# A vision-transformer layer on one core: the class product of the class query's weighted sum moved behind the four token products

## The chip, the cores and the metric

One core of a Trainium2 chip runs the whole program. The metric is the device time of one execution in microseconds; the median of several executions is compared.

## The reference

Sixteen images of 512 tokens with 256 features pass through one layer. The changed lines belong to the attention, whose core is, cut to what matters:

```python
h = concatenate([broadcast(cls_tok), tok(x)], axis=1)      # 513 rows an image
...
q, k, v = bitlinear(x, w_q), bitlinear(x, w_k), bitlinear(x, w_v)   # 16 heads of 16
scores = einsum('bhqd,bhkd->bhqk', q, k) * SCALE
attn = softmax(scores, axis=-1)
out = einsum('bhqk,bhkd->bhqd', attn, v)
...
h = h + bitlinear(out, w_o)
h = h + moe_top2(layernorm(h))                              # 8 experts
```

The class token is row 0 of each image. As a query it attends to the 512 tokens and to itself. Its output is a sum over 512 token keys and one class key, weighted by exponentials of the scores, divided by the sum of the weights.

## The kernel before

The program has two large parts. The first, which the change touches, takes the images through a software pipeline: gate and up projections, attention, router. The second goes over the experts' token lists and follows behind a barrier.

In the first part five images are in flight. One turn of the pipeline has 64 steps (four groups of four heads, 16 units each; `at` counts the steps, `u` the units of a group). In a turn the functions `body` of the engines hand over `T, P, C, W, X`: image T is in the token projections, P in the attention's projections, C in the score maxima, W at the end of its attention, X in the output projection and the router. The order of the work on each engine is written out by hand by these step numbers; the engines wait for each other through semaphores alone. Turns 3 to 12 are a hardware loop with two turns in its body, the others are straight code.

Each step of `tensor_program` begins with a score product of 512 keys (`score_unit`, line 493), whose row maximum VectorE takes (`head_max`, line 1147) into `mxs`, and a transposed score product (`scoret_unit`, line 502), whose exponential ScalarE takes into `pt` (line 823). The score products alternate between two PSUM banks, so TensorE can be one or two units ahead of VectorE. The attention's products `pv` (line 511) come every fourth step: four heads, each with 32 output columns, write the four strips of 32 partitions of one bank.

At step 35 the class query's weighted sum of image W stands (lines 737 to 743). `pc` holds the exponentials: 32 columns (16 heads and padding) for each of four tiles of 128 tokens, and in place `TB` one row for the class key. `v_sb` holds the values of a tile, 16 heads by 32 columns, `vcls` those of the class token. The product of token tile t goes into partitions 32t to 32t + 31 of PSUM bank `d2`; the class key's product, of one row, is added into the strip of tile 0. All are float32, and each is executed in two passes (two records in the trace). The last of the five raises `pe_pvc`.

```python
for t in range(TB):
    last = mm(d2[VW * t:VW * (t + 1), :], pc[:, W.par, t, :], ...)
    if t == 0:
        mm(d2[0:VW, :], pc[0:1, W.par, TB, :], vcls[0:1, W.par, :, :]...)
last.then_inc(s("pe_pvc"), 1)
```

At step 36 VectorE, behind its row maximum, waits for `pe_pvc` and multiplies the whole bank by the mask `diagonal` into `pvd` (line 1436). TensorE's transposes of the attention's output into the same bank, `d2`, wait for that at step 38 (line 635). At step 44 line 750 sums the four strips. On VectorE step 35 also has a piece of the router of image X (lines 1241 to 1243, on masks `rtmp` and `oh`), at step 41 another (lines 1241 to 1246) and at step 42 the router's weights (lines 1255 to 1257). GpSimd runs the low parts of the queries and keys of image P by step numbers of its own: line 1021 and line 1025 at step 35, line 1029 at step 42, each some 2 us.

Of the kernel before, what the change touches and what calls it, by code (L numbers as in the profile page):

```python
# [19 lines left out]
TB = S // 128  # L20
# [6 lines left out]
VW = 32  # L27
# [70 lines left out]
def fresh(eng, at, *batches):  # L98

    if batches[0].n is None or isinstance(batches[0].n, int):  # L100
        return batches
    n = batches[0].n
    copy = eng.alloc_register(f"lap_{batches[0].k}_{at}")
    eng.reg_mov(copy, n)
    n = eng.snap(copy, min_val=n.min_val, max_val=n.max_val)
    return [At(b.k, n, b.ok) for b in batches]


def wait(eng, sem, per, b, n):

    value = b.v * per + n
    if not isinstance(value, int) or value > 0:
        eng.wait_ge(sem, value)
# [31 lines left out]
def token_phase(nc, outer, images, x_t, cls, w0_t, w1_t, wo_t, attn_w_t, gate_w, consts, out,  # L145
# [12 lines left out]
    def s(name):  # L158

        if name not in sems:  # L160
            sems[name] = nc.alloc_semaphore(f"{name}_{stage}")
        return sems[name]
# [101 lines left out]
    vcls = sb("vcls", [128, 2, NH, VW])  # L264
# [4 lines left out]
    pc = sb("pc", [128, 2, TB + 1, VW])  # L269
# [51 lines left out]
    d0, d1, d2 = banks[5:8]  # L321
# [143 lines left out]
    def tensor_program(pe, stage):  # L465
        mm, tr = nc.tensor.matmul, nc.tensor.transpose
        if stage == SETUP:
# [8 lines left out]
            for c in range(DC):  # L476
                last = mm(d1[:, 4 + c:5 + c], cls_norm[:, blk(c)], ones[0:1, 0:1], start=True, stop=True)
# [37 lines left out]
        def body(T, P, C, W, X):  # L515
            for g in range(NG):
                for u in range(UNITS):
                    if u % 4 == 0:
                        T, P, C, W, X = fresh(pe, UNITS * g + u, T, P, C, W, X)
# [10 lines left out]
                    if T.ok and at in GATE_AT:  # L530
# [10 lines left out]
                        for c in range(DC):  # L541
                            last = mm(d0[:, :], w0[:, c, blk(e)], xt[:, T.par, c, :], start=(c == 0), stop=(c == DC - 1))  # L542
                        last.then_inc(s("pe_gate"), 1)
                    if T.ok and at in UP_AT:
# [7 lines left out]
                        for c in range(DC):  # L552
                            last = mm(d1[:, :], w1[:, c, blk(e)], xt[:, T.par, c, :], start=(c == 0), stop=(c == DC - 1))
                        last.then_inc(s("pe_up"), 1)
                    if T.ok and at in OUT_AT:
                        t = OUT_AT.index(at)
# [4 lines left out]
                        for e in range(EC):  # L561
                            last = mm((d0, d1)[t // 2][:, D * (t % 2):D * (t % 2 + 1)], hid[:, e, blk(t)], wo[:, e, :],
                                      start=(e == 0), stop=(e == EC - 1))
                        if t % 2:
                            last.then_inc(s("pe_h"), 1)
                    if C.ok and at == 0:
# [4 lines left out]
                        for c in range(DC):  # L571
                            mm(d2[:, 0:D], xq[:, c, S:SEQ].broadcast_to([128, 128]), wq_int[:, 2, c, :],
                               start=(c == 0), stop=(c == DC - 1))
                        for w in range(2):
                            for f in range(DC):
                                for c in range(DC):
                                    last = mm(d2[:, D + 2 * w + f:D + 2 * w + f + 1], wq_int[:, w, c, blk(f)],
                                              xq[:, c, S:SEQ], start=(c == 0), stop=(c == DC - 1))
                        last.then_inc(s("pe_cols"), 1)
                    if X.ok and at == 1:  # L580
# [5 lines left out]
                        for c in range(DC):  # L586
                            for t in range(TB):
                                last = tr(b16(d0)[:, c * S + t * 128:c * S + (t + 1) * 128], qi2[:, t, blk(c)], id_bf[:, :])
                        last.then_inc(s("pe_xq2"), 1)
                        tr(b16(d1)[0:64, 0:NG], qic[:, :], id_bf[0:NG, 0:NG]).then_inc(s("pe_xqc"), 1)  # L590
                    if C.ok and at == 3:
# [3 lines left out]
                        for k, (a, o) in enumerate(((fq, kbd), (fk, qbd))):  # L595
                            for half in range(2):
                                for c in range(DC):
                                    last = mm(d2[VW * (2 * k + half):VW * (2 * k + half + 1), 0:S // 2], o[:, c, :],
                                              a[:, c, half * S // 2:(half + 1) * S // 2], start=(c == 0), stop=(c == DC - 1))
                        last.then_inc(s("pe_ct"), 1)  # L600
                    if X.ok and at in (4, 5):
# [5 lines left out]
                        for t in (2 * k, 2 * k + 1):  # L607
                            for c in range(DC):
                                last = mm((d0, d1)[k][:, D * (t % 2):D * (t % 2 + 1)], xq2[:, c, blk(t)],
                                          wq_int[:, 3, c, :], start=(c == 0), stop=(c == DC - 1))  # L610
                            last.then_inc(s("pe_y"), 1)
                    if u == 6 and tg[0].ok:
# [21 lines left out]
                        for t in range(TB):  # L634
                            last = tr(d2[:, blk(t)], pvs[:, blk(t)], identf)
                        last.then_inc(s("pe_tg"), 1)
                    if u == 9 and mt[0].ok:
# [8 lines left out]
                        for t in range(TB):  # L646
                            last = tr(b16(d2)[0:MROWS * GH, blk(t)], nmp[:, t, :], id_bf[:, :])
                        last.then_inc(s("pe_mt"), 1)
                    if P.ok and at == 10:
                        wait(pe, s("act_xh"), TB, P, TB)  # L650
                        wait(pe, s("dve_sst"), 1, P, 1)
                        if X.ok:
                            wait(pe, s("dve_h2"), TB, X, TB)
                        mm(d1[:, 0:2 * TB], ones[:, :], sums1[:, :, :].rearrange("p a t -> p (a t)"),
                           start=True, stop=True).then_inc(s("pe_st1"), 1)
                    if C.ok and at == 12:
# [6 lines left out]
                        for c in range(DC):  # L663
                            last = mm(d2[:, S // 2:S // 2 + NH], fq[:, c, S:SEQ].broadcast_to([128, 128]),
                                      kbd[:, c, 0:NH], start=(c == 0), stop=(c == DC - 1))
                        wait(pe, s("dve_cm"), 1, C, 1)
                        mm(d2[:, CM_AT:CM_AT + 2 * VW], cm[:, 0:1].broadcast_to([128, 128]), cst[:, C_ID + 2 * VW:C_ID + 4 * VW],
                           start=True, stop=True).then_inc(s("pe_t7"), 1)
                    if X.ok and at == 9:
                        hold(pe, s("dve_h2"), TB, X, 2)  # L670
                        for k in range(NG):
                            last = mm(d0[0:1, 0:D], xqc[:, k:k + 1], wo_cls[:, k, :], start=(k == 0), stop=(k == NG - 1))
                        last.then_inc(s("pe_yc"), 1)
                    if P.ok and at == 24:
# [5 lines left out]
                        for t in range(TB):  # L680
                            last = mm(d1[:, blk(t)], aq1[:, t:t + 1].broadcast_to([128, 128]), identf, start=True, stop=True)
                        last.then_inc(s("pe_aqb"), 1)
                    if P.ok and at == 23:
# [5 lines left out]
                        for c in range(DC):  # L689
                            for t in range(TB):  # L690
                                last = tr(b16(d0)[:, c * S + t * 128:c * S + (t + 1) * 128], qi[:, t, blk(c)], id_bf[:, :])
# [8 lines left out]
                    if X.ok and at in (28, 30):  # L700
# [9 lines left out]
                        for t in range(TB):  # L710
                            last = tr(d2[:, blk(t)], x2[:, t, blk(c)], identf)
# [3 lines left out]
                    if P.ok and at in (41, 42):  # L715
# [7 lines left out]
                        for t in (2 * k, 2 * k + 1):  # L723
                            for c in range(DC):
                                last = mm((d0, d1)[k][:, D * (t % 2):D * (t % 2 + 1)], xq[:, c, blk(t)],
                                          wq_int[:, 2, c, :], start=(c == 0), stop=(c == DC - 1))
# [3 lines left out]
                    if W.ok and at == 35:  # L730

                        wait(pe, s("act_pc"), 1, W, 1)
                        if X.ok:
                            wait(pe, s("dve_lg"), 1, X, 1)
                        else:
                            wait(pe, s("act_mt"), NG, C, 1)
                        for t in range(TB):
                            last = mm(d2[VW * t:VW * (t + 1), :], pc[:, W.par, t, :],
                                      v_sb[:, W.par, t, :, :].rearrange("p h w -> p (h w)"), start=True, stop=(t > 0))
                            if t == 0:  # L740
                                mm(d2[0:VW, :], pc[0:1, W.par, TB, :], vcls[0:1, W.par, :, :].rearrange("p h w -> p (h w)"),
                                   start=False, stop=True)
                        last.then_inc(s("pe_pvc"), 1)
                    if W.ok and at == 44:

# [3 lines left out]
                        for k in range(NG):  # L749
                            last = mm(d2[0:NG, 0:GH * VW], cst[:, C_SEL + k * NG:C_SEL + (k + 1) * NG],  # L750
                                      pvd[:, k * GH * VW:(k + 1) * GH * VW], start=(k == 0), stop=(k == NG - 1))
# [9 lines left out]
                    if W.ok and at == 56:  # L761
# [4 lines left out]
                           start=True, stop=True).then_inc(s("pe_amc"), 1)  # L766
# [31 lines left out]
        if stage == STEPS:  # L798
            steps(pe, body)
# [1058 lines left out]
```

## Time and profile before

| | |
|---|---|
| three runs | 2411.87, 2416.78, 2420.08 us (median 2416.78) |
| profiled execution | span 2410.7 us; no time of its own beside the span is listed |
| granted TensorE clock, mean | 0.955 |
| TensorE busy | 2081.0 us (86%) |
| VectorE busy | 1571.5 us (65%) |
| ScalarE busy | 1210.0 us (50%) |
| GpSimd busy | 911.2 us (38%) |

The span runs from the first to the last instruction of the program. Lines L1 to L1857 are the lines of the kernel. PE is TensorE, DVE VectorE, ACT ScalarE, POOL GpSimd. A timeline gives the start of an instruction, its duration, engine, line, operation, what it writes and reads, the shapes, and in brackets how long the engine sat idle ahead of it and what ended that. Instructions of one line in a row are merged (x2, x8). Matmuls overlap, so their cost is read from start to start. A granted clock of 1.00 is 2.4 GHz, 0.50 is 1.2 GHz.

### The profile page before, as it was taken

What the parts mean: (1) busy time and instruction counts of PE and PEld (TensorE: products, weight loads), DVE (VectorE), ACT (ScalarE), POOL (GpSimd) and SP (SyncE); (2) the same over time, 40 slices, a digit from 0 to 9 for tenths busy, and PEclk for the clock granted to TensorE, in tenths of its full rate; (3) what the DMA queues carried; (4) which work ended last, traced back from release to release, by engine and by line L of the source; (5) the groups of instructions that cost most, each with busy time, mean ns of one, the idle gap of its engine ahead of it and who ended that gap; (6) DMA issues with size and microseconds to landing.
All of it is one profiled execution on the core that took longest, in us unless ns stands there. A gap on an engine that the chain in (4) does not pass through costs nothing. (4 is left out here: it accounts for less than half of the span.)

```text
span 2410.7 us, 46759 instructions
## 1 busy us (share of the span) xinstructions
PE 2081.0 (86%) x11964; PEld 1058.4 (44%) x12049; DVE 1571.5 (65%) x4036; ACT 1210.0 (50%) x2360; POOL 911.2 (38%) x894
## 2 busy tenths in 40 slices
PE   4889999999898898998998988861099999999997
PEld 2433444444343444443444433321066666666665
DVE  3477888887887887887888898841633333333332
ACT  1256566566565565665656666640444444444443
POOL 2222242332423423333234244133245555555554
PEclk9899999999999999999999998985599999999999
DMA  2322332322222323223232232201523333333332
GB/s 99 83 74 53 86 87 69 93 71 81 85 71 68 87 69 88 77 70 87 69 78 82 65 85 74 64 27 45 191 45 57 53 56 54 53 56 52 55 54 37
DMA packets 181071, 171.97 MB, mean 71 GB/s; under 512 B 40002, under 2 KB 169620, under 8 KB 180884
## 3 DMA queue, kind: packets, MB, share of 16 engines
q1 hardware_dynamic: 150612, 134.94, 20.1%
q0 software_dynamic: 30272, 34.80, 9.1%
q8 instruction: 86, 1.41, 0.3%
q14 instruction: 101, 0.83, 0.2%
HBM read 100.82 MB, written 68.93 MB: 70 GB/s over the span
## 5 line engine op out<-in xcount | busy, mean ns | idle before, releaser
L1147 DVE TENSOR_REDUCE mxs<-bank 128x1 f32<-128x512 f32 x1024 | 697.1, 685 | 205.0 <-PE bank L493 186.5
L823 ACT ACTIVATE pt<-bank 128x512 f32<-128x512 f32 x1024 | 588.5, 593 | 388.8 <-PE bank L502 369.3
L493 PE MATMUL bank<-ks,qs 96*128 96x512 bf16 x1024 | 397.9, 390 | 84.1 <-DVE mxs L1147 53.3
L502 PE MATMUL bank<-qs,ks 99*128 99x512 bf16 x1024 | 393.4, 385 | 9.2 <-ACT pt L823 8.7
L1697 POOL DMA_INDIRECT out<-y_sb,ids x136 | 214.6, 1578 | 273.3 <-DMA out<-y_sb,ids 193.7
L511 PE MATMUL bank<-pt,v_sb 128*32 128x512 f32 x2048 | 278.0, 615 | 0.0
L493 PEld LDWEIGHTS bank<-ks,qs 96*128 96x128 bf16 x1024 | 103.1, 101 | 357.5 <-DVE mxs L1147 214.0
L1826 DVE TENSOR_TENSOR hl<-bank,hh 128x512 bf16<-128x512 f32 x136 | 94.1, 692 | 210.7 <-ACT hh L1796 210.7
L1822 DVE TENSOR_TENSOR hid_e<-bank,act_g 128x512 f32<-128x512 f32 x136 | 94.1, 692 | 210.5 <-PE bank L1743 209.0
L974 POOL DMA_INDIRECT list_dram<-pay,slot_i x130 | 138.3, 1064 | 240.9 <-DVE pay L1272 206.7
L1743 PE MATMUL bank<-gu_l,xh 128*128 x544 | 206.9, 380 | 22.9 <-issue 21.2
L1743 PE MATMUL bank<-gu_h,xl 128*128 x543 | 206.6, 380 | 0.0
L991 POOL TENSOR_TENSOR cadd<-vcls,pr 128x256 f32<-128x256 f32 x64 | 41.1, 642 | 400.3 <-DVE pr L1194 400.0
L1743 PE MATMUL bank<-gu_h,xh 128*128 x477 | 181.9, 381 | 2.0 <-issue 1.2
L1688 POOL DMA_INDIRECT xg<-x_dram,ids x136 | 135.8, 998 | 64.7 <-issue 36.9
L1728 PE MATMUL bank<-dn_h,hh 128*128 x544 | 148.4, 273 | 3.0 <-DVE hl L1826 1.6
L1728 PE MATMUL bank<-dn_h,hl 128*128 x544 | 148.3, 273 | 0.0
L1728 PE MATMUL bank<-dn_l,hh 128*128 x544 | 148.3, 273 | 0.0
L502 PEld LDWEIGHTS bank<-qs,ks 99*128 99x128 bf16 x1024 | 100.2, 98 | 98.8 <-issue 38.6
L1789 ACT ACTIVATE act_g<-bank 128x512 f32<-128x512 f32 x136 | 81.2, 597 | 122.8 <-PE bank L1743 121.9
L542 PE MATMUL bank<-xt,w 128*128 128x512 f32 x256 | 130.8, 635 | 7.7 <-DMA xt<-x_t 7.7
L1784 ACT ACTIVATE y_sb<-bank,ids 128x256 f32<-128x256 f32 x136 | 64.3, 473 | 141.5 <-PE bank L1728 121.7
(283 smaller groups left out, 3529.2 us busy)
## 6 DMA issues: line engine op xcount, KB each, us to landing
qs<-qk_dram SPq DMA_DIRECT2D x128, 128.0 KB, 2.6
ks<-qk_dram SPq DMA_DIRECT2D x64, 192.0 KB, 3.4
xt<-x_t SPq DMA_DIRECT2D x16, 512.0 KB, 4.2
h_dram<-h_sb SPq DMA_DIRECT2D x16, 512.0 KB
qs<-qk_dram SPq DMA_DIRECT2D x128, 64.0 KB, 2.2
ks<-qk_dram SPq DMA_DIRECT2D x64, 128.0 KB, 3.4
hw<-h_dram SPq DMA_DIRECT2D x16, 512.0 KB, 4.3
out<-hw SPq DMA_DIRECT2D x16, 512.0 KB, 2.9
```

Of the source, the lines that this page charges most:

```text
L493: mm(score[u % 2][:, :], qs[0:QK, h, blk(t)], ks[0:QK, h, :], start=True, stop=True) \
L502: mm(scoret[u % 2][:, :], ks[0:QK + MROWS, h, blk(t)], qs[0:QK + MROWS, h, :], start=True, stop=True).then_inc(s("pe_st"), 1)
L511: last = mm(pv_bank[VW * j:VW * (j + 1), :], v_sb[:, b.par, t, g * GH + j, :], pt[:, t % 2, j, :], start=(t == 0), stop=(t == TB - 1))
L542: last = mm(d0[:, :], w0[:, c, blk(e)], xt[:, T.par, c, :], start=(c == 0), stop=(c == DC - 1))
L823: f(pt[:, t % 2, j, :], scoret[u % 2][:, :], ACT.Exp).then_inc(s("act_exp"), 1)
L974: g_.indirect_dma_start(out=list_dram, out_offset=bass.IndirectOffsetOnAxis(ap=slot_i[0:np_, k, t:t + 1], axis=0), in_=pay[0:np_, k, t, :] ...
L1147: v.reduce_max(mxs[:, t, g * GH + j:g * GH + j + 1], score[u % 2][:, :], AX.X).then_inc(s("dve_mx"), 1)
L1688: nc.gpsimd.indirect_dma_start(out=xg[:, i.place(ROWS), :], out_offset=None, in_=x2_dram, in_offset=rows(i)) \
L1697: nc.gpsimd.indirect_dma_start(out=out, out_offset=rows(i), in_=y_sb[:, i.place(2), :], in_offset=None, bounds_check=tokens - 1, oob_is_er ...
L1728: last = mm(y_b[:, 0:D], a[:, i.place(2), c, :], w[:, bass.ds(e, 1), c, :], start=(n == 1), stop=(n == 3 * FC))
L1743: last = mm(bank[k][:, :], a[:, k, c, :], w[:, bass.ds(e, 1), c, lo:lo + F], start=(m == 1), stop=(m == 3 * DC))
L1822: v.tensor_tensor(hid[:, :], up_b[i.place(2)][:, :], act_g[:, :], ALU.mult).then_inc(dve_hid, 1)
```

## The change

The class key's product is issued after the four token products instead of after the first, and raises `pe_pvc` in place of the product of tile 3. Operands, shapes and the accumulation flags of each product stay.

```diff
                         for t in range(TB):
                             last = mm(d2[VW * t:VW * (t + 1), :], pc[:, W.par, t, :],
                                       v_sb[:, W.par, t, :, :].rearrange("p h w -> p (h w)"), start=True, stop=(t > 0))
-                            if t == 0:
-                                mm(d2[0:VW, :], pc[0:1, W.par, TB, :], vcls[0:1, W.par, :, :].rearrange("p h w -> p (h w)"),
-                                   start=False, stop=True)
+                        last = mm(d2[0:VW, :], pc[0:1, W.par, TB, :], vcls[0:1, W.par, :, :].rearrange("p h w -> p (h w)"),
+                                  start=False, stop=True)
                         last.then_inc(s("pe_pvc"), 1)
```

On TensorE, at steps 35 and 36 in the loop's body, before (L738 is the token products, L741 the class product, L104 and L113 are bookkeeping of the loop's registers):

```order
L511 MATMUL bank<-pt,v_sb 32x512 x4
L738 MATMUL bank<-v_sb,pc 32x512
L741 MATMUL bank<-vcls,pc 32x512
L738 MATMUL bank<-v_sb,pc 32x512 x3
L104 ISA
L493 MATMUL bank<-ks,qs 128x512
L113 REGISTER_ALU
L502 MATMUL bank<-qs,ks 128x512
```

and with the change (lines behind the edit have moved up by one, the class product is L740):

```order
L511 MATMUL bank<-pt,v_sb 32x512 x4
L738 MATMUL bank<-v_sb,pc 32x512 x4
L740 MATMUL bank<-vcls,pc 32x512
L104 ISA
L493 MATMUL bank<-ks,qs 128x512
L113 REGISTER_ALU
L502 MATMUL bank<-qs,ks 128x512
```

The four token products now stand together behind the four of the attention, and the class product stands between them and the score product of step 36.

On TensorE in the last image, where no score products are left, before (L780 is the router's logits, L635 the transposes that wait for `pvd`):

```order
L780 MATMUL bank<-gate_sb,x_t 128x8 x8
L511 MATMUL bank<-pt,v_sb 32x512 x4
L738 MATMUL bank<-v_sb,pc 32x512
L741 MATMUL bank<-vcls,pc 32x512
L738 MATMUL bank<-v_sb,pc 32x512 x3
L635 MATMUL bank<-cst,pvs 128x128 x4
```

and with the change:

```order
L779 MATMUL bank<-gate_sb,x_t 128x8 x8
L511 MATMUL bank<-pt,v_sb 32x512 x4
L738 MATMUL bank<-v_sb,pc 32x512 x4
L740 MATMUL bank<-vcls,pc 32x512
L635 MATMUL bank<-cst,pvs 128x128 x4
```

Here the class product is the one that stands directly ahead of the transposes. On the other engines no instruction moves.

## Rows read from the trace of the kernel before

**Rows 1.** The page's head: span, then busy time, share and instructions.

```profile
span 2410.7 us, 46759 instructions
...
PE 2081.0 (86%) x11964; PEld 1058.4 (44%) x12049; DVE 1571.5 (65%) x4036; ACT 1210.0 (50%) x2360; POOL 911.2 (38%) x894
```

**Rows 2.** Timeline of PE at steps 35 and 36 of one image.

```profile
602.38 1.06 PE L511 MATMUL bank<-pt,v_sb 128*32 128x512 f32 x8
603.26 1.02 PE L738 MATMUL bank<-v_sb,pc 128*32 128x512 f32 x2
604.21 1.04 PE L741 MATMUL bank<-vcls,pc 1*32 1x512 f32 x2
605.18 1.06 PE L738 MATMUL bank<-v_sb,pc 128*32 128x512 f32 x6
606.17 0.39 PE L493 MATMUL bank<-ks,qs 96*128 96x512 bf16 x1
```

**Rows 3.** Stretches: length, PE, PEld, DVE, ACT, POOL busy, clock, DMA; sum over 16.

```profile
603.26:606.17 2.91, 2.91 (x14) 0.39 (x10) 2.84 (x3) 0.70 (x2) 2.73 (x2) 1.00 0.08 26
...
1464.26:1467.82 3.56, 3.56 (x15) 0.47 (x10) 3.13 (x3) 0.60 (x1) 3.01 (x2) 0.82 0.03 10
1542.50:1545.41 2.91, 2.91 (x14) 0.39 (x9) 1.01 (x4) 0.60 (x1) 0.00 (x0) 1.00 0.48 163
...
sum 47.21, PE 47.21 PEld 6.37 DVE 38.69 ACT 11.80 POOL 38.62; mean PE 2.95 PEld 0.40 DVE 2.42 ACT 0.74 POOL 2.41
```

**Rows 4.** Timeline of DVE at steps 35 to 37 of the image of rows 2.

```profile
604.42 2.05 DVE L1243 TENSOR_TENSOR oh<-cst,ix 128x32 f32<-128x32 f32 x1
606.65 0.69 DVE L1147 TENSOR_REDUCE mxs<-bank 128x1 f32<-128x512 f32 x1 [0.18 <-PE bank L493]
...
608.75 0.69 DVE L1147 TENSOR_REDUCE mxs<-bank 128x1 f32<-128x512 f32 x1 [0.82 <-PE bank L493]
609.36 0.18 DVE L1232 SCALAR_TENSOR_TENSOR lg<-oh,lg 128x32 f32<-128x32 f32 x1
```

**Rows 5.** Waits, whole span: who waited for whom, us in total, times, longest.

```profile
DVE mxs L1147 <- PE bank L493: 186.5, 265, 4.9
...
PE bank L493 <- DVE mxs L1147: 53.3, 91, 1.6
```

**Rows 6.** Timeline of POOL beside rows 4.

```profile
604.29 2.12 POOL L1025 TENSOR_TENSOR rest<-fk,part_kh 128x1024 f32<-128x1024 f32 x1 [0.18 <-POOL part_ql L1021]
```

**Rows 7.** Timeline of DVE at steps 35 and 36 of a late image.

```profile
1465.45 2.01 DVE L1243 TENSOR_TENSOR oh<-cst,ix 128x32 f32<-128x32 f32 x1
1468.31 0.69 DVE L1147 TENSOR_REDUCE mxs<-bank 128x1 f32<-128x512 f32 x1 [0.85 <-PE bank L493]
```

**Rows 8.** Timeline of PE behind the last image's weighted sum.

```profile
1613.65 0.63 PE L635 MATMUL bank<-cst,pvs 128*128 128x128 f32 x4 [0.95 <-DVE pvd L1436]
```

**Rows 9.** Timeline of PE around steps 43 to 45, two images.

```profile
618.27 0.39 PE L493 MATMUL bank<-ks,qs 96*128 96x512 bf16 x1 [1.62 <-DVE mxs L1147]
...
713.85 0.39 PE L493 MATMUL bank<-ks,qs 96*128 96x512 bf16 x1 [0.36 <-DVE mxs L1147]
```

**Rows 10.** Timeline of DVE in these images; last, line 1246: durations minimum/median/maximum in ns.

```profile
615.56 2.06 DVE L1246 TENSOR_TENSOR picked<-oh 128x32 bf16<-128x32 f32 x1
...
710.04 0.19 DVE L1246 TENSOR_TENSOR picked<-oh 128x32 bf16<-128x32 f32 x1
...
711.16 1.82 DVE L1257 TENSOR_TENSOR wts<-e21e,wts 128x4 f32<-128x4 f32 x1
...
L1246 DVE TENSOR_TENSOR picked<-oh x17: 153/2053/2060, 327.9 to 1702.1; 128x32 bf16<-128x32 f32 x16, 16x8 bf16<-16x8 f32 x1
```

**Rows 11.** Stretches from one image's weighted sum to the next, columns as in rows 3.

```profile
603.26:698.58 95.32, 87.76 (x501) 39.44 (x498) 80.93 (x220) 57.11 (x113) 33.51 (x39) 1.00 0.27 76
893.32:991.94 98.62, 89.34 (x500) 40.47 (x497) 79.62 (x220) 57.06 (x113) 33.48 (x39) 0.97 0.28 77
698.58:798.01 99.43, 90.49 (x500) 40.29 (x497) 79.52 (x220) 57.08 (x113) 33.57 (x39) 0.95 0.29 80
```

## The prediction

> **What bounds the kernel now.** I read the page's head first, then the timeline of TensorE (PE) around the changed products, then VectorE's (DVE) and GpSimd's (POOL) over the same microseconds, and last the stretches that say how far one image differs from the next. The page gives PE 2081.0 us busy of 2410.7 [rows 1]. A share over the whole span says little about five matmuls, so the question is whether PE is what the others wait for where they stand.
>
> In PE's timeline the reader is to see starts, not durations, since matmuls overlap. The weighted sum's five products are three blocks in a row: tile 0 at 603.26, the class key's product at 604.21, tiles 1 to 3 at 605.18, and the next score product at 606.17 [rows 2]. That is 0.95 + 0.97 + 0.99 = 2.91 us, with no idle time on PE before any of them. Each product is two records (x2, x2, x6), so three products in three strips of 32 output partitions cost about what one product alone costs. The attention's own four products ahead of them fill all four strips, and from their start at 602.38 to tile 0 it is 0.88 us [rows 2]: four strips cost one block as well.
>
> All 16 images do this: 15 stretches are 2.91 us and fully PE-busy, the one at 1464.26 is 3.56 at a granted clock of 0.82, together 47.21 us [rows 3]. After the group DVE is the one that waits: 0.18 us before the row maximum of step 36 and 0.82 before that of step 37, both times for PE's score product [rows 4]. So here PE sets the pace. Over the whole program the two engines take turns: DVE's maxima waited 186.5 us for PE's scores, PE's scores 53.3 us for the maxima [rows 5].
>
> **The change, part by part.** It removes no instruction and adds none. The class product moves behind tiles 1 to 3, and with it the signal that DVE's masking product waits for. PE issues no DMA here and no wait is added; the rows on DVE, ScalarE, POOL and SyncE stay as they are.
>
> *The four tile products.* With tile 0 beside tiles 1 to 3, four strips share one block. Its price lies between 0.95, a block that ends in front of the class product, and 0.99, a block that ends in front of a score product [rows 2]. I take 0.97.
>
> *The class product.* It still runs alone: it writes strip 0, which tile 0 has just written. Its price lies between 0.97, as now, and 0.99, when a score product follows [rows 2]. I take 0.97.
>
> *Together* 1.94 us instead of 2.91, so PE gains **0.97 us per image**, with bounds of 0.93 (1.98 now needed) and 0.99 (1.92).
>
> *What of it reaches the end.* PE goes on at once with the score products of step 36, so all of it arrives at DVE's maxima. DVE can only use what it waits: 0.18 + 0.82 = 1.00 us [rows 4]. In front of step 36 it can gain no more than 0.18, because its mask of expert indices (line 1243) took 2.05 us and ended at 606.47, right behind POOL's operation of 604.29 to 606.41 [rows 4, 6], and POOL's does not depend on the changed products. The rest comes at step 37: DVE would be through with the masking product early enough, and its maximum moves from 608.75 to 607.78. The gain fits into the 1.00, with 0.03 to spare; from there on PE and DVE are late together, and a still faster PE group would give nothing more. POOL's next operation and ScalarE's exponentials follow DVE and PE, so the next steps move up as a whole.
>
> Three images are different. At 1464.26 DVE has no wait of 0.82 behind it: its mask ends at 1467.46 and the maximum starts at 1468.31, so 0.85 is all that can be won [rows 7]. At 1542.50 DVE is busy for 1.01 us in the group, so it isn't held and the whole 0.97 arrives [rows 3]. At the last image PE itself waits 0.95 us for the masking product before its next transposes [rows 8]; the signal comes 0.97 earlier and so does everything behind it.
>
> Sum: 15 x 0.97 + 0.85 = **15.4 us**; with the bounds 14.8 to 15.7. The profiled span goes from 2410.7 to about 2395.3. The three runs gave 2411.87 to 2420.08 with a median of 2416.78, which is 6.1 above that span, so the forecast is 2416.8 - 15.4 = **2401.4 us**, 0.64% faster.
>
> **A rule weighed.** The rows show that the class product and tiles 1 to 3 do not overlap: 0.97 us between their starts [rows 2]. The Trainium skill, "TensorEngine Tiling (Array Packing)", Key Properties, says that tiles of the array operate independently and may run matmuls in parallel; by that alone the class product in strip 0 would already run beside tiles 1 to 3, the group would be two blocks before and after, and the change would be worth nothing. The same section says that changing the tiling mode, as opposed to the tile, drains the engine, and a one-row product among 128-row ones is such a change; with that sentence the trace agrees, by the 0.97 us.
>
> **The rivals.**
>
> *DVE takes part of it.* The margin of 0.03 us at step 37 is thin. If DVE's start behind POOL's operation costs a little more than now, or the wait reappears at one of PE's waits for the maxima some steps later, then between a third and two thirds survive: 5 to 10 us, 2407 to 2412. For it speaks that DVE is busy 2.84 of the 2.91 us [rows 3]; against it, that both waits in [rows 4] are for PE, and that what follows is either PE's or waits for PE.
>
> *Two blocks now, or three then.* If the class product already streamed beside tiles 1 to 3, the group would be two blocks in either order; if tile 0 kept a block of its own behind the attention's products, it would be three in either order. Both give 2416.8. Against the first speaks that the score product starts 2.91 us, three blocks, after tile 0, against the second that four strips took 0.88 us [rows 2]. The first is what the independence of tiles, in the Trainium skill's section named above, would give.
>
> *Slower by a new collision.* DVE's small operations on SBUF last until the end of a POOL operation when they meet one: the last mask of the router (line 1246) took 2.06 us at 615.56, and in another image a weight product (line 1257) took 1.82 at 711.16 [rows 10], against 0.19 for line 1246 unhindered. Which one is hit already changes from image to image, and PE then waits 1.62 or 0.36 us [rows 9]. Moving DVE up by 0.97 could put one more operation per image under POOL's: 2.05 - 0.19 = 1.86 us lost in each of the 13 images that have both the router's and the projections' image in flight beside them, 24.2 us, less the 15.4 gained is 8.8 us slower, 2425.6. It decides from a new loss of (15.4 + 7.3)/13 = 1.75 us per image. Against it: DVE's next such operations come after 609.36, 2.95 us behind the end of POOL's [rows 4, 6], and move by 0.97 only; POOL's next one starts after DVE's own result and moves along.
>
> *Other gains or losses of that kind.* If the images that lose 1.62 us and those that lose 0.36 swap, each is worth 1.26 us; the median of line 1246's 17 is 2.05 us [rows 10], so at least nine of the 13 lose the larger amount and at most four the smaller: +5 to -11 us. The clock is smaller: an image at a granted clock of 1.00 (2.4 GHz) took 95.32 us, those with a turn of the loop and some microseconds at half of it 98.62 (mean 0.97) and 99.43 (0.95) [rows 11], so 0.81 us between two depths of the drop, over four turns some 3 us either way.
>
> **How the numbers follow.** A measurement of this kernel tells about 0.3%, 7.3 us, from no change. Full gain, 13 to 18 us: 0.74. More than that, with collisions falling well: 0.05. A part through DVE: 0.11, half of it over 7.3 us. Nothing: 0.06. Slower: 0.04. Faster by over 0.3% is 0.74 + 0.05 + 0.06 = 0.85, within 0.3% is 0.05 + 0.06 = 0.11, slower 0.04. The range: below the forecast by about 8 us for collisions and clock, 2393; above it up to where half of the gain is lost, 2410.
>
> **What would show it.** In the new profile PE's timeline has the tile products as one block of x8, the class product's x2 0.95 to 0.99 later and the score product 1.92 to 1.98 after the start. DVE's wait before the maximum of step 36 is gone and that of step 37 is below 0.15 us. An image at full clock without a turn of the loop takes about 94.35 us instead of 95.32. The prediction is wrong if the group still takes over 2.5 us, if PE's waits for the maxima in steps 37 to 43 grow by more than 0.3 us per image, or if more small DVE operations last 1.8 us and over.

## The result, and the profile after

The changed kernel took 2398.60 us (median of five runs, 2395.59 to 2404.18), the kernel before 2416.78 us (median of its five runs, 2409.41 to 2420.08). The ratio is 0.9944, with an interval of 0.9924 to 0.9965: faster by 0.35 to 0.76%. The forecast of 2401.4 us is a ratio of 0.9936 and lies inside. The profiled execution took 2398.6 us with a span of 2396.8, where before's span is 2410.7 [rows 1]: 13.9 us less.

The page's head of the changed kernel:

```profile
span 2396.8 us, 46843 instructions
...
PE 2081.3 (87%) x12048; PEld 1056.4 (44%) x12049; DVE 1572.6 (66%) x4036; ACT 1213.0 (51%) x2360; POOL 912.7 (38%) x894
```

TensorE's busy sum is what it was, although the span is shorter. The two sums can't be compared: before's trace lacks 84 matmul records that the new one has (11964 against 12048 [rows 1]), 68 of them of one line in the second part. In the changed line the busy time does fall: the token products (L738) take 33.9 us over the program before and 16.7 now. What the change is worth is read from starts. The timeline of TensorE at steps 35, 36 and 41 of the image that answers to [rows 2]:

```profile
599.97 1.06 PE L511 MATMUL bank<-pt,v_sb 128*32 128x512 f32 x8
600.85 1.04 PE L738 MATMUL bank<-v_sb,pc 128*32 128x512 f32 x8
601.82 1.04 PE L740 MATMUL bank<-vcls,pc 1*32 1x512 f32 x2
602.80 0.39 PE L493 MATMUL bank<-ks,qs 96*128 96x512 bf16 x1
...
608.83 0.39 PE L493 MATMUL bank<-ks,qs 96*128 96x512 bf16 x1 [0.43 <-DVE mxs L1146]
```

Two blocks instead of three: tile 0 stands with the other tiles (x8), the class product comes 0.97 us later and the score product 1.95 after the start. In all 15 images with a score product behind it the group now takes 1.94 to 1.95 us; in the last image the transposes of L635 start 2.95 us after it, 3.93 before, with an idle 0.93 us in between (0.95 before). Stretches of three groups and of two images, with the columns of [rows 3]:

```profile
600.85:602.80 1.95, 1.95 (x15) 0.27 (x7) 1.88 (x3) 0.71 (x2) 1.77 (x2) 1.00 0.12 42
1452.87:1454.81 1.94, 1.94 (x14) 0.26 (x7) 1.94 (x2) 1.25 (x4) 1.90 (x1) 1.00 0.49 173
1532.17:1534.11 1.94, 1.94 (x14) 0.26 (x6) 1.01 (x4) 0.60 (x1) 0.00 (x0) 1.00 0.70 242
600.85:695.33 94.48, 86.88 (x502) 39.24 (x498) 81.11 (x220) 57.22 (x113) 33.60 (x39) 1.00 0.27 76
...
888.73:987.03 98.30, 88.86 (x501) 40.29 (x497) 80.80 (x220) 57.29 (x113) 33.52 (x39) 0.97 0.29 81
```

An image at full clock without a turn of the loop takes 94.48 us where it took 95.32 [rows 11]: 0.84 won, not 0.97. Where most of the 0.13 went is seen on VectorE, at steps 35 to 37 of the same image (lines behind the edit stand one lower here, so L1242 is line 1243 of the kernel before; from the experiments on, the text names lines by their numbers before):

```profile
602.03 2.05 DVE L1242 TENSOR_TENSOR oh<-cst,ix 128x32 f32<-128x32 f32 x1
604.26 0.69 DVE L1146 TENSOR_REDUCE mxs<-bank 128x1 f32<-128x512 f32 x1 [0.18 <-DVE oh L1242]
604.87 0.68 DVE L1435 TENSOR_TENSOR pvd<-bank,cst 128x512 f32<-128x512 f32 x1
605.47 0.68 DVE L1146 TENSOR_REDUCE mxs<-bank 128x1 f32<-128x512 f32 x1
```

and GpSimd's operation beside them:

```profile
601.91 2.13 POOL L1024 TENSOR_TENSOR rest<-fk,part_kh 128x1024 f32<-128x1024 f32 x1 [0.18 <-POOL part_ql L1020]
```

The mask of line 1242 still lasts until GpSimd is done (604.08 against 604.04), and the 0.18 us ahead of the maximum of step 36 is still there, now put down to that mask and not to TensorE. That maximum starts 3.41 us after the group's start, as before (3.39). The maximum of step 37 starts at once behind the masking product, 4.62 us after the group's start; before it was 5.49 [rows 2, 4]. In the nine other images with the same wait of 0.18 it is 4.58 to 4.62 instead of 5.50. So 0.88 to 0.92 arrives there, and VectorE alone is then the late one. At step 41 TensorE's wait is 0.43 us here and 0.40 or 0.41 in most, where it had been 0.35.

The two waits of [rows 5], over the whole span:

```profile
DVE mxs L1146 <- PE bank L493: 173.5, 242, 3.4
...
PE bank L493 <- DVE mxs L1146: 66.2, 110, 2.0
```

VectorE waits 13.0 us less for the scores; at steps 36 and 37 alone it is 14.8 less (21.6 before, 6.7 now). The 12.9 us more that TensorE's row shows are a matter of names. All of its idle time ahead of the score products is 84.1 us before and 83.3 now, by the page before and the page after:

```profile
L493 PE MATMUL bank<-ks,qs 96*128 96x512 bf16 x1024 | 397.9, 390 | 84.1 <-DVE mxs L1147 53.3
```

```profile
L493 PE MATMUL bank<-ks,qs 96*128 96x512 bf16 x1024 | 399.2, 391 | 83.3 <-DVE mxs L1146 66.2
```

At steps 62 and 63 before's trace puts 12.7 us of it down to "issue", that is to nothing that it shows, and the new one puts all of it down to the maxima. From the first group's start to the last scatter of the image part the trace shows 14.7 us less. The rest of the 13.9 lies outside it: the first group starts 2.4 us later (228.23 against 225.81), and the stretch behind the image part is 1.7 us shorter.

### The profile page after: what moved, and what is told of

Read it like the earlier page. It is cut to its first block and busy times, and to the rows that moved or that the text cites. A ratio compares the mean times of both kernels' runs of the same rounds, so it can differ in the third digit from the quotient of the medians.

```text
span 2396.8 us, 46843 instructions
## 1 busy us (share of the span) xinstructions
PE 2081.3 (87%) x12048; PEld 1056.4 (44%) x12049; DVE 1572.6 (66%) x4036; ACT 1213.0 (51%) x2360; POOL 912.7 (38%) x894
## 5 line engine op out<-in xcount | busy, mean ns | idle before, releaser
L493 PE MATMUL bank<-ks,qs 96*128 96x512 bf16 x1024 | 399.2, 391 | 83.3 <-DVE mxs L1146 66.2
L1742 PE MATMUL bank<-gu_h,xh 128*128 x544 | 208.3, 383 | 11.3 <-issue 8.2
```

The costliest lines, as they stand in the source:

```text
L493: mm(score[u % 2][:, :], qs[0:QK, h, blk(t)], ks[0:QK, h, :], start=True, stop=True) \
L1742: last = mm(bank[k][:, :], a[:, k, c, :], w[:, bass.ds(e, 1), c, lo:lo + F], start=(m == 1), stop=(m == 3 * DC))
```

## The experiments

Theory A: the class product stands apart because its shape on the array is another (one row among 128-row products). Theory B: because of the strip it writes. For the later runs the theory is that VectorE, held by GpSimd, sets the pace behind the group, so that only VectorE's work is worth moving.

**The order of before, class product of 128 rows.** The class key then counts 128 times, so the output differs in that part.

```diff
-mm(d2[0:VW, :], pc[0:1, W.par, TB, :], vcls[0:1, W.par, :, :]...)
+mm(d2[0:VW, :], pc[:, W.par, TB, :], vcls[:, W.par, :, :]...)
```

> The order of before (tile 0, class product, tiles 1 to 3), but the class product has 128 rows instead of one, so that all five products have the same tile shape; the class key then counts 128 times. Theory A (a change between 128-row and one-row products separates the blocks): tile 0 costs 0.86 to 0.89 us, the class product runs beside tiles 1 to 3 in one block of 0.99, so the group takes about 1.87 us, and the time is that of the changed kernel, ratio to before 0.992 to 0.997. Theory B (the class product separates because it must follow tile 0 in the same strip, and everything behind it waits until it is through): 2.91 us and a ratio of 0.997 to 1.003.

Measured: 2397.96 us against 2414.15, ratio 0.9939 (0.9922 to 0.9956). Its timeline of TensorE:

```profile
602.56 1.06 PE L738 MATMUL bank<-v_sb,pc 128*32 128x512 f32 x8
603.42 1.02 PE L741 MATMUL bank<-vcls,pc 128*32 128x512 f32 x2
604.38 0.39 PE L493 MATMUL bank<-ks,qs 96*128 96x512 bf16 x1
```

The tiles share a block although the class product is issued between them, and the group takes 1.82 us. Tile 0 was expected alone and the class product beside tiles 1 to 3; instead all four tiles stand together and the class product follows them. The order alone was never the obstacle; the shape was. That is A.

**The order of before, one-row class product in the strip of tile 3.**

```diff
-mm(d2[0:VW, :], pc[0:1, W.par, TB, :], vcls[0:1, W.par, :, :]..., start=False, stop=True)
+mm(d2[3 * VW:4 * VW, :], pc[0:1, W.par, TB, :], vcls[0:1, W.par, :, :]..., start=True, stop=False)
```

Tile 3's product then adds to it.

> The order of before, the class product with its one row, but written into the strip of tile 3 instead of that of tile 0; tile 3 is added onto it. The sum over the four strips is the same. Theory A (change of the tile shape): still three blocks, 2.91 us from tile 0 to the next score product, ratio 0.997 to 1.003. Theory B (same strip): the class product runs beside tile 0 or beside tiles 1 and 2, two blocks, 1.9 to 2.0 us, ratio 0.992 to 0.997.

Measured: 2411.52 us against 2414.15, ratio 0.9992 (0.9982 to 1.0003). TensorE:

```profile
603.84 1.02 PE L738 MATMUL bank<-v_sb,pc 128*32 128x512 f32 x2
604.79 1.04 PE L741 MATMUL bank<-vcls,pc 1*32 1x512 f32 x2
605.77 1.06 PE L738 MATMUL bank<-v_sb,pc 128*32 128x512 f32 x6
606.76 0.39 PE L493 MATMUL bank<-ks,qs 96*128 96x512 bf16 x1
```

Three blocks, although the class product has a strip that tile 0 doesn't use. B falls.

**The changed kernel with a class product of 128 rows**, the edit of the first run on the new order (a single run, so without an interval).

> The order of the change, with a class product of 128 rows; the class key counts 128 times. Theory A: without a change of the shape the class product follows 0.86 to 0.89 us after tile 0 instead of 0.97, the group takes 1.83 to 1.88 us instead of 1.94. Theory B: 1.94 us as with one row.

Measured: 2396.95 us in its one run. The class product starts 0.86 us after the tiles and the group takes 1.81 us, but in the ten images with the wait of 0.18 ahead of step 36 the maximum of that step starts at 3.37 to 3.39 and that of step 37 at 4.58 or 4.59 us after the start: what TensorE gains now isn't passed on there.

**The changed kernel once more**, beside the next three runs.

> The changed kernel once more, beside the next three: a ratio to before of 0.992 to 0.997, group of 1.94 us, and in the images in which VectorE's mask of step 35 is held by GpSimd the maximum of step 36 about 3.4 us after tile 0.

Measured: 2402.35 us (2393.55 to 2408.91) against 2415.79, ratio 0.9953 (0.9939 to 0.9967).

**The class product in four quarters, one per strip.** Each quarter of 128 columns (four heads) is added in another strip; step 44 sums the strips anyway.

```diff
-last = mm(d2[0:VW, :], pc[0:1, W.par, TB, :], vcls[0:1, W.par, :, :]...)
+for t in range(TB):
+    last = mm(d2[VW * t:VW * (t + 1), blk(t)], pc[0:1, W.par, TB, :], vcls[0:1, W.par, heads(t), :]...)
```

> The changed kernel, with the class product cut into four products of 128 columns, one in each strip (line 750 sums the strips, so the result stays). They can share a block: the class part falls from 0.97 to about 0.35 us and the group from 1.94 to about 1.3. Theory (VectorE, held by GpSimd at step 35, already sets the pace behind the group): the 0.6 us per image come back as longer waits of TensorE for the maxima within some steps, and the time is that of the changed kernel within 3 us. Rival (TensorE still sets the pace): 16 x 0.6 = 10 us less than the changed kernel, a ratio of about 0.990 to before.

Measured: 2406.57 us, ratio 0.9966 (0.9952 to 0.9979). TensorE, then VectorE, in one image:

```profile
607.93 1.04 PE L738 MATMUL bank<-v_sb,pc 128*32 128x512 f32 x8
608.91 0.42 PE L741 MATMUL bank<-vcls,pc 1*32 1x128 f32 x8
609.26 0.39 PE L493 MATMUL bank<-ks,qs 96*128 96x512 bf16 x1
...
615.89 0.39 PE L493 MATMUL bank<-ks,qs 96*128 96x512 bf16 x1 [0.49 <-DVE mxs L1147]
```

```profile
609.09 2.05 DVE L1243 TENSOR_TENSOR oh<-cst,ix 128x32 f32<-128x32 f32 x1
611.32 0.69 DVE L1147 TENSOR_REDUCE mxs<-bank 128x1 f32<-128x512 f32 x1 [0.18 <-DVE oh L1243]
...
612.52 0.68 DVE L1147 TENSOR_REDUCE mxs<-bank 128x1 f32<-128x512 f32 x1
```

The group takes 1.33 us, 0.62 less, and the maxima start 3.39 and 4.59 us after its start, as in the changed kernel. TensorE's wait at step 41 is 0.49. A faster group gains nothing here. The time is 4.2 us above the repeated run, more than the 3 that were expected, but the two intervals overlap. This execution had more holds, too: line 1246 in all 13 images, in the repeated run in 8.

**The router's pieces 0 and 1 both at step 34**, ahead of GpSimd's operations, in the changed kernel.

```diff
-ROUTER_AT = (34, 35, 37, 41)
+ROUTER_AT = {34: (0, 1), 37: (2,), 41: (3,)}
```

> The changed kernel, with the router's piece of step 35 moved to step 34, behind the one that stands there, so that it is over before GpSimd's operation begins. The mask of line 1242 takes 0.2 us instead of 2.05. Theory: VectorE's maximum of step 36 starts about 2.4 us after tile 0 instead of 3.4, but TensorE's score product limits that of step 37 to 4.53 instead of 4.59: at most 0.06 us per image, 1 us in all, no change that can be measured. Rival (VectorE's hold at step 35 is the bound by itself): up to 0.9 us per image, 12 us less than the changed kernel.

Measured: 2402.07 us, ratio 0.9943 (0.9929 to 0.9956). VectorE:

```profile
603.69 0.69 DVE L1146 TENSOR_REDUCE mxs<-bank 128x1 f32<-128x512 f32 x1 [2.67 <-PE bank L493]
604.30 0.68 DVE L1435 TENSOR_TENSOR pvd<-bank,cst 128x512 f32<-128x512 f32 x1
605.85 0.69 DVE L1146 TENSOR_REDUCE mxs<-bank 128x1 f32<-128x512 f32 x1 [0.86 <-PE bank L493]
```

Now VectorE is early and waits 2.67 and 0.86 us for TensorE; the maximum of step 37 starts 4.53 us after the group's start. Freeing VectorE alone is worth no more than the 0.06 by which it had been late. (In three of the images outside the loop the mask still takes 2.12 to 2.18 us at step 34, without making the maxima late.)

**Both edits together.**

> Both edits: the class product in four quarters and the router's piece at step 34. Theory: each has taken away what hid the other, so together they give what neither gives alone, 0.6 to 0.7 us in 13 to 16 images, 8 to 11 us less than the changed kernel, ratio to before about 0.990. Rival (a later wait, such as the one of step 41 or that for the exponentials, takes it back): the time of the changed kernel.

Measured: 2396.36 us, ratio 0.9924 (0.9910 to 0.9938): 6.0 us under the repeated run of the changed kernel, where 8 to 11 were expected. The maximum of step 37 starts 3.91 us after the group's start, 0.62 earlier than with the router's edit alone, the expected step. Part of what lacks is given back later: in all 13 images the last mask (line 1246) meets GpSimd's operation of line 1029, and TensorE waits at step 44, 1.61 or 1.62 us in ten of them and 1.02 in three; in the repeated run the mask was held in 8 of 13. The images with a turn of the loop took 99.0 to 100.6 us against 96.4 to 97.5; the profiled execution of the repeated run was the fastest of its five, 2393.55, so this second comparison says less. VectorE and then TensorE:

```profile
612.00 2.05 DVE L1246 TENSOR_TENSOR picked<-oh 128x32 bf16<-128x32 f32 x1
```

```profile
614.71 0.39 PE L493 MATMUL bank<-ks,qs 96*128 96x512 bf16 x1 [1.62 <-DVE mxs L1147]
```

**The router's last piece at step 39, its weights at step 45**, in the kernel with both edits.

```diff
-ROUTER_AT = {34: (0, 1), 37: (2,), 41: (3,)}
+ROUTER_AT = {34: (0, 1), 37: (2,), 39: (3,)}
...
-if X.ok and at == 42:
+if X.ok and at == 45:
     weights(X, "", TB, 128)
```

> The run before (e7_both) with the router's piece 3 at step 39 instead of 41 and its weights at step 45 instead of 42, away from GpSimd's operation of line 1029. Theory (VectorE, dense and partly held by GpSimd from step 37 to 46, is what TensorE waits for there): the last mask operation of line 1246 lasts 0.2 us in all 13 images instead of 2.05, TensorE's wait of 1.62 us at step 44 falls under 0.4, but the piece lengthens VectorE's work ahead of step 41 by 0.8 us, so that 0.8 to 1.3 us per image are left: 10 to 17 us under e7_both, a ratio to the kernel before of 0.985 to 0.988. Rival (the stretch is set by something else, such as TensorE's own work): the time of e7_both, 0.991 to 0.994.

Measured: 2382.31 us against 2415.45, ratio 0.9871 (0.9853 to 0.9889): 14.1 us under the run before. Line 1246 lasts 0.19 us on average, and the wait of 1.62 is gone; the piece's own time comes back as a longer wait at step 41 (0.68 before), as expected:

```profile
605.48 0.39 PE L647 MATMUL bank<-id_bf,nmp 128*12 128x128 bf16 x4 [1.46 <-DVE o_sb L1193]
```

**Piece 2 behind the masking product of step 36, piece 3 at step 38, weights at step 45**, with the class product in quarters.

```diff
-ROUTER_AT = {34: (0, 1), 37: (2,), 39: (3,)}
+ROUTER_AT = {34: (0, 1), 38: (3,)}
...
 v.tensor_tensor(pvd[:, :], d2[:, :], diagonal, ALU.mult)...
+if X.ok and at == 36:
+    router(X, "", TB, 128, pieces=(2,))
```

> As e7_both, but the router's piece 2 stands behind the masking product of step 36, where VectorE waits 0.87 us for TensorE, piece 3 at step 38 and the weights at step 45. Theory: VectorE's dense stretch loses the 0.8 us of piece 2 and some 2.7 us in which GpSimd held piece 3; TensorE's waits of 0.35, 0.68 and 1.62 us in steps 40 to 44 mostly go, 1.5 to 2.5 us per image, 20 to 33 us under e7_both, a ratio of 0.979 to 0.984. Rival: piece 2, held until GpSimd's operation ends, delays the maximum of step 37 by about 1 us, and what is won later is lost here: a ratio of 0.988 to 0.993.

Measured: 2371.66 us, ratio 0.9823 (0.9808 to 0.9838): 24.7 us under the kernel with both edits. **The same with the class product as one block**, as in the changed kernel:

> The places of e9_slots, but with the class product as one block behind the four tile products, as in the changed kernel, so the group takes 1.94 us instead of 1.32. Theory: where VectorE no longer sets the pace from step 37 on, a faster group pays: this kernel is slower than e9_slots by up to 0.62 us in each of 13 to 16 images, 5 to 10 us, 0.002 to 0.004 in the ratio. Rival (VectorE still sets the pace): no difference, under 0.0015.

Measured: 2377.02 us, ratio 0.9844 (0.9829 to 0.9859). VectorE in the first of the two:

```profile
598.80 0.25 DVE L1232 SCALAR_TENSOR_TENSOR lg<-oh,lg 128x32 f32<-128x32 f32 x1
...
602.22 0.19 DVE L1246 TENSOR_TENSOR picked<-oh 128x32 bf16<-128x32 f32 x1
```

Piece 2 now stands in a hole in which VectorE waited; its first operation is held for a moment (0.25 us instead of 0.18). Beyond that, pieces 2 and 3 and the weights are held in no image; the mask at step 34 still is in three images outside the loop (2.12 to 2.17 us). One full-clock image without a turn of the loop, in the kernel with both edits, then in the one with the places and quarters, then with the places and one block:

```profile
601.28:695.00 93.72, 86.24 (x507) 39.24 (x503) 78.41 (x219) 57.09 (x113) 33.45 (x39) 1.00 0.27 76
```

```profile
595.85:687.30 91.45, 86.02 (x507) 39.23 (x503) 75.94 (x219) 56.94 (x113) 33.45 (x39) 1.00 0.29 80
```

```profile
596.95:689.03 92.08, 86.64 (x502) 39.21 (x498) 75.89 (x219) 56.93 (x113) 33.44 (x39) 1.00 0.29 79
```

VectorE's busy time falls by 2.47 us per image, the image by 2.27. And between the last two, with VectorE out of the way, the 0.62 us of the quarters arrives in full: 91.45 against 92.08. The intervals of their ratios overlap by a little. The images without a turn of the loop don't (the eight at full clock are each 0.60 to 0.64 us shorter with the quarters); those with one do, 96.8 to 99.2 us with the quarters and 95.6 to 98.7 without. The kernel with places and quarters beats both kernels of this study.

## Why the prediction was right, point by point

*Blocks.* Right. The class product at 0.97 and the group at 1.94 to 1.95 were forecast as 0.97 and 1.94. That it stands apart by its shape is shown: with 128 rows in the old place two blocks, with one row in another strip three. The forecast's own reason, that the class product writes the strip which tile 0 has just written, suffices in the new order (with 128 rows it still follows 0.86 us behind the tiles), but it isn't what made three blocks of the old: in another strip the class product stood apart just the same. Two sentences of the Trainium skill, "TensorEngine Tiling (Array Packing)", Key Properties, had been weighed. The one on independent tiles doesn't hold here for a one-row product among 128-row ones. The one on a change of mode fits, if another number of rows counts as another mode; the page doesn't say that, and that the engine drains isn't shown, only that the blocks don't overlap. Of the rival, "two blocks now" is refuted by [rows 2] and "three then" by the new timeline.

*The wait of 0.18 us ahead of step 36.* Wrong. "In front of step 36 it can gain no more than 0.18" was a safe bound, but "DVE's wait before the maximum of step 36 is gone" failed: the 0.18 follows the held mask in either order. Before, TensorE's score product and the mask ended close together, and the view named the wrong one of the two. In the first image of before, where no mask is held, the score product lets this maximum start 3.34 us after the group's start; the held mask makes it 3.39.

*The gain fits with 0.03 to spare.* Wrong in size. With the 0.18 not to be had, only the wait of 0.82 and what VectorE's chain allows remain: the maximum of step 36 at 3.39, two operations of some 0.60 us, the maximum of step 37 at 4.59, 0.91 us earlier than 5.50. The rival "DVE takes part of it" was thus true, for some 0.06 us instead of the third to two thirds that it was given. TensorE's wait at step 41 grew by that same 0.06, from 0.35 to 0.41: this is how the loss reaches TensorE, not a second loss. From there to step 60 its score products start 0.89 to 0.92 us earlier; from step 66, that is step 2 of the next turn, the lead is 0.83 to 0.88. What takes the last 0.05 was not followed up.

*Exceptions.* At 1542.50 the whole 0.97 arrives, as forecast: the maximum of step 37 starts 3.65 us after the group's start instead of 4.62. The first image and those at 317.73 and 1366.68 show the 0.97 there, too (4.53 instead of 5.50). At the last image TensorE still waits 0.93 us for the masking product, so its gain passes on, as forecast. The image at 1464.26 was called worth 0.85. Its group now runs at full clock, but its mask is held until 4.22 us after the group's start (3.20 before) and TensorE then waits 2.01 us at step 38 (0.20 before), so that the intervals on its two sides moved by -1.39 and +1.07.

*The sum.* 15.4 us forecast, 14.7 measured over the image part, and part of this nearness is luck. The images at full clock and without a turn of the loop in which line 1246 fared alike in both traces gained 0.83 to 0.99 us. In two others line 1246 was held before and is not now, and they gained 1.92 and 1.90. One of them, before and after:

```profile
1186.13:1281.46 95.33, 87.79 (x500) 39.43 (x497) 81.07 (x220) 57.10 (x113) 33.44 (x39) 1.00 0.28 76
```

```profile
1179.95:1273.36 93.41, 86.88 (x501) 39.24 (x497) 80.05 (x220) 57.20 (x113) 33.64 (x39) 1.00 0.28 77
```

Whether that line is held makes 1.07 us per image (94.48 against 93.41 in the changed kernel), where the forecast had counted 1.26 for a swap. Three images lost the hold and two got it, so one such 1.07 is in the 14.7. The images with a turn of the loop gained anything from 0.3 to 2.0 us. The medians differ by 18.2 us; over two sets of five runs whose own spread is 8.6 and 10.7 us that says no more than the interval. The repeated run gave 2402.35, 13.4 below the runs of before that stood beside it.

*"A still faster PE group would give nothing more."* Right, and shown twice: by the quarters (group 1.33 us, maxima where they were) and by the later places, where with VectorE freed the same 0.62 us counts in full in the full-clock images.

*Slower by a new collision.* It didn't come: line 1246 was held in nine images and line 1257 in four, afterwards in eight and five. TensorE's waits for the maxima at steps 37 to 43, which the forecast named as a sign, grew from 4.4 to 6.8 us over 15 images, 1.8 of it in the image at 1452.87.

What stays open: why the images with a turn of the loop vary (96.4 to 97.5 us in one run, 99.0 to 100.6 in another). Two parts are on record, the mean granted clock (0.965 to 0.982 in the first, 0.949 to 0.966 in the second) and the holds of line 1246 (one of the four images in the first, all in the second); no run tried the rest. Nor was it tried what each of the three moves in the places is worth by itself, beyond the two runs shown.

## What to carry to other kernels

Among matmuls that fill separate strips of the array, a product of another height, here one row among 128, ended the overlap on both sides: put it at an end of the row, not in the middle, or give it the height of the others. Before you count a wait as the room for a gain, ask what would end last if the engine named had been done earlier. When a gain stops at an engine that another one holds, move the held operations into stretches in which that engine waits: here this was worth more than the change itself.

## What had not been expected of the hardware

Here a class product over 128 rows costs less than one over a single row: its start comes 0.86 us after the tiles instead of 0.97, and the group takes 1.81 us instead of 1.94.

In these traces a VectorE operation on two SBUF operands that starts during one of GpSimd's operations of some 2 us ends with it: 2.05 us for lines 1243 and 1246 (numbers of the kernel before) where the same operation unhindered takes 0.19, while operations that read PSUM, and the statistics over one SBUF operand, keep their times of 0.68 and 0.69 beside GpSimd. The Trainium skill, "SBUF — State Buffer", section "SBUF: two separate sides", has the rule: an operation of VectorE with two SBUF inputs and one of GpSimd that reads SBUF exclude each other, and whichever starts first keeps the other out for its whole length. The rows agree for the case that GpSimd is first. What was not expected is its weight: moving the router's last piece and its weights out of GpSimd's reach, and piece 2 into a hole of VectorE, took the time from 2396.36 to 2371.66 us.
